# Probabilities times values in four column tiles of 32 tokens instead of two of 64, in a gated linear attention and expert layer

## What is computed

```python
A = jnp.einsum('bhntd,bhnsd->bhnts', q, k)
A = A * jnp.where(mask, jnp.exp(jnp.where(mask, dec, 0.0)), 0.0)
o_intra = jnp.einsum('bhnts,bhnsd->bhntd', A, v)
...
def step(S, inp):
    o_int = jnp.einsum('bhtd,bhde->bhte', qc * jnp.exp(gcc)[..., None], S)
...
o = o_intra + jnp.moveaxis(o_inter, 0, 2)
```

## Time and profile before

| | |
|---|---|
| median of 3 runs | 410.85 us (409.74 to 411.74) |
| the profiled execution, its time | 410.52 us |
| its span, first to last instruction | 408.6 us |
| mean granted TensorE clock | 0.991 |
| PE busy | 386.7 us, 3650 MATMULs |
| PEld busy | 337.1 us |
| DVE busy | 326.3 us |
| ACT busy | 304.5 us |
| POOL busy | 276.6 us |

### The profile page before, as it was taken

The page is one execution under the profiler, slowest core; times in us unless marked ns, Lnnn a source line. Parts: engine busy times, 40 slices in busy tenths (PEclk is TensorE's granted clock), DMA queues, the critical chain, the costliest instruction groups (busy, mean ns, idle before and its releaser), DMA issues.

```text
span 408.6 us, 13495 instructions
## 1 busy us (share of the span) xinstructions
PE 386.7 (95%) x3650; PEld 337.1 (83%) x3651; DVE 326.3 (80%) x868; ACT 304.5 (75%) x947; POOL 276.6 (68%) x237
## 2 busy tenths in 40 slices
PE   7988899999999999999999999899999999999990
PEld 6656788877788888888888878799999999999990
DVE  5989898999988898889888888667687687687750
ACT  4889998787887978797888887466666676666660
POOL 6012534268888888888888833178888888888884
PEclk9999999999999999999999999999999999999996
DMA  8846586464555445474655340145545555455530
GB/s 237 230 158 193 177 288 245 120 186 129 170 179 162 128 127 168 143 200 140 186 155 154 115 137 14 44 63 69 69 68 65 66 69 67 63 67 71 64 32 0
DMA packets 59096, 51.29 MB, mean 126 GB/s; under 512 B 7200, under 2 KB 51392, under 8 KB 59072
## 3 DMA queue, kind: packets, MB, share of 16 engines
q1 hardware_dynamic: 45936, 42.07, 36.0%
q0 software_dynamic: 12272, 8.54, 15.1%
q10 hardware_dynamic: 864, 0.40, 0.4%
HBM read 33.14 MB, written 18.30 MB: 126 GB/s over the span
## 4 chain that ended last, share of the span: by engine, by line
PE 80%; DVE 6%; ACT 4%; DMA 3%; issue 3%; POOL 2%; SPq 1%; ACTq 0%; DVEq 0%; POOLq 0%
PE psA L912 16%; PE psVG L900 16%; PE psVG L721 9%; PE psO L756 8%; PE psA L737 7%; PE psT L790 6%; PE psQK L709 6%; PE psT L782 4%; PE psKS L747 3%; PE psO L770 3%; ACT E L1080 2%; SPq L343 1%; DMA x_all<-in_L_attn_x_dram 1%; DMA gcB<-decay_rows 1%; PE psQK L891 1%
## 5 line engine op out<-in xcount | busy, mean ns | idle before, releaser
L579 POOL DMA_INDIRECT out_dram<-yw,sidx x71 | 115.0, 1619 | 29.1 <-issue 11.6
L538 POOL TENSOR_TENSOR rms<-msn,neg_half 128x8 f32<-128x8 f32 x32 | 53.3, 1665 | 48.4 <-DVE msn L1412 44.7
L1080 ACT ACTIVATE E<-gcB,ngc 128x128 f32<-128x128 f32 x256 | 78.5, 397 | 0.4 <-DMA gcB<-decay_rows 0.4
L544 POOL DMA_INDIRECT sorted_rows<-x_all,pos_i x64 | 65.2, 1019 | 14.4 <-issue 10.5
L531 POOL TENSOR_SCALAR_AFFINE_SELECT E<-E 128x1024 f32<-128x1024 f32 x32 | 35.7, 1115 | 33.5 <-ACT E L1080 33.2
L756 PEld LDWEIGHTS psO<-v_sb,pr 128*64 128x64 f32 x1024 | 39.8, 137 | 12.0 <-issue 4.1
L756 PE MATMUL psO<-v_sb,pr 128*64 128x64 f32 x1024 | 44.5, 225 | 2.7 <-DVE pr L1440 2.5
L1089 ACT ACTIVATE sq<-psO 128x512 f32<-128x512 f32 x32 | 19.1, 597 | 33.4 <-PE psO L756 33.4
L1440 DVE TENSOR_TENSOR pr<-psA,E 128x512 f32<-128x512 f32 x64 | 41.0, 682 | 0.2
L912 PE MATMUL psA<-xT_all,v_sb 128*128 x288 | 38.3, 276 | 0.5 <-issue 0.4
L900 PE MATMUL psVG<-xgT,gcB 128*128 128x128 f32 x288 | 38.6, 277 | 0.0
(11 more groups left out here) (197 smaller groups left out, 928.5 us busy)
## 6 DMA issues: line engine op xcount, KB each, us to landing
gcB<-decay_rows SPq DMA_DIRECT2D x32, 512.0 KB
sorted_rows<-blank SPq DMA_DIRECT2D x12, 396.0 KB, 5.5
xg<-sorted_rows SPq DMA_DIRECT2D x71, 66.0 KB
x_all<-in_L_attn_x_dram SPq DMA_DIRECT2D x16, 256.0 KB, 5.3
out_dram<-res SPq DMA_DIRECT2D x32, 128.0 KB
eqB<-decay_exp_rows SPq DMA_DIRECT2D x32, 64.0 KB
w1b<-in_L_ffn_w_dram SPq DMA_DIRECT2D x8, 256.0 KB
xT_all<-in_L_ffn_w_dram SPq DMA_DIRECT2D x32, 64.0 KB
```

What stands on the lines that cost most here:

```text
L538: nc.gpsimd.tensor_tensor(rms[:], msn[:], neg_half[:, 0:2 * H], ALU.pow).then_inc(rms_ready, 1)
L544: nc.gpsimd.indirect_dma_start(out=sorted_dram, out_offset=bass.IndirectOffsetOnAxis(ap=pos_i[:, t:t + 1], axis=0), in_=x_all[:, t, :], in ...
L579: nc.gpsimd.indirect_dma_start(out=out_rows, out_offset=bass.IndirectOffsetOnAxis(ap=sidx[j][:], axis=0), in_=yw[j][:], in_offset=None, bo ...
L1080: last = nc.scalar.activation(E[j][:, k, h * P:(h + 1) * P], gcB[j][:, k * H + h, :], ACT.Exp, bias=ngcf[:, bass.ds((s * 2 + k) * H + h, 1)])
```

## The change

A constant `QT = 4` is added, and the two loops over token tiles run over `QT` tiles of 32 tokens instead of 2 of 64. Each head of each chunk is then 4 matmuls instead of 2, and the state's part is 4 instead of 2; each still streams the same number of columns, against 32 columns of weights instead of 64. Nothing else is changed, waits and increments neither.

```diff
     LS = P // GT
+    QT = 4
...
                 for h in range(H):
-                    for c in range(2):
-                        t = k * SEQ + h % 2 * P + c * P // 2
-                        last = nc.tensor.matmul(psO[c * P // 2:(c + 1) * P // 2, k * HV + h * DV:k * HV + (h + 1) * DV], pr[:, h // 2, t:t + P // 2],
+                    for c in range(QT):
+                        t = k * SEQ + h % 2 * P + c * P // QT
+                        last = nc.tensor.matmul(psO[c * P // QT:(c + 1) * P // QT, k * HV + h * DV:k * HV + (h + 1) * DV], pr[:, h // 2, t:t + P // QT],
                                                 v_sb[j][:, k, h * DV:(h + 1) * DV], start=(k == 0 and h == 0), stop=(k == 1 and h == H - 1),
                                                 skip_group_check=True)
...
-                for c in range(2):
-                    nc.tensor.matmul(psO[c * P // 2:(c + 1) * P // 2, HV:2 * HV], qe[j][:, c * P // 2:(c + 1) * P // 2], S_sb[:],
+                for c in range(QT):
+                    nc.tensor.matmul(psO[c * P // QT:(c + 1) * P // QT, HV:2 * HV], qe[j][:, c * P // QT:(c + 1) * P // QT], S_sb[:],
                                      start=False, stop=False, skip_group_check=True)
```

## The result

The changed kernel took **428.7 us** (427.7 to 429.5, 4 runs) against 411.3 us (409.7 to 412.1, 4 runs) of the kernel before on the same chip: a ratio of 1.043, 95% interval 1.040 to 1.046. The forecast was 410.4 us and its range ended at 424, so both were missed.

What follows compares the result with a forecast made beforehand. PE's own time was taken as the bound; 29 ns gained on weight loads less 14 ns for a later end gave 0.5 us over 32 sequences, added starts costing nothing: 410.4 us, range 408.5 to 424.

Steps and rivals of the forecast that it cites:

- What bounds the kernel: In the attention stage PE's own time is the bound, so its gain or loss reaches the total almost one for one.
- Part (1): In each half of the outputs, 16 added MATMULs and 16 LDWEIGHTS cost zero; a step stays at 58 ns.
- (2): In the state's part, 4 more MATMULs and LDWEIGHTS cost zero, hidden under 208 ns of stream for each pass.
- (3): At a burst's first step, narrower weights load in 108 ns instead of 137, giving back 29 ns once a sequence.
- C: Rival: in the outputs' steps, 6 ns of overhead vanish with narrower weights, 3 us in all, 407 us; chance 0.10.
- rival B: Pauses in the outputs' long bursts come earlier or double, +2 to +13 us, 412.5 to 424 us; chance 0.35.

Runs made afterwards that it cites:

- second measurement: The unedited changed kernel timed again on another chip, against the kernel before there: 408.6 us, ratio 0.997 (0.995 to 0.999).
- 10: The kernel before (two tiles) with the state's part streamed as two pieces of 128 columns: 410.1 us, ratio 1.001.
- 12: The kernel before (two tiles), with GpSimd placing one tile, awaiting DVE's norming, masking, then placing two: 406.7 us, ratio 0.994.
- 15: The kernel before (two tiles) with 16 instead of 8 warm-up matmuls, which shifts TensorE's later code: 411.3 us, ratio 1.005.
- experiment 3: The changed kernel (four tiles) with GpSimd's mask after one placement and the other two placements behind it: 426.7 us, ratio 1.036.
- 4: The kernel before (two tiles) with GpSimd's mask after one placement and the other two placements behind it: 414.7 us, ratio 1.009.
- group 1: Four follow-up runs on one chip, without placing or with the mask moved, each on four and two tiles; the kernel before took 411.3 us there.

## Why the prediction was wrong, and where it was right

**What bounds the kernel**: right. What TensorE lost in the outputs came onto the total almost one for one: 20.8 us of longer periods, 20.1 between the medians.

**Part (1), added starts at nothing**: right. Quiet sequences on every chip show 32 MATMULs in 0.58 and 0.45 us; a step of four takes 56 ns, against 58 for a pair. The floor of about 25 ns between starts that the prediction cites from the Trainium skill (TensorE: Matmul & The Clock Gate, Back-to-back issue gap), and sets aside, would have made it 100; the trace's starts lie 7 ns apart. **(2)** and **(3)** were right too: 0.43 us for the state's part, loads of 111 ns. **C** had a grain of truth: a step got 2 ns shorter, of the 6 that it forecast. With part (3) the period is 0.07 us shorter (6.89 to 6.82). In 32 sequences this is 2.3 us, and the second measurement shows 0.7 us of it in the medians, its ratio's interval reaching to 0.995; where the other 1.6 went wasn't followed. So without the pauses the forecast of no change, 410.0 for 410.5, was right.

**The step that failed** is rival B: the sum put pauses at nothing, and B's own price ended at +13 us. Its sentence "If the pause ends at a given time, as much more of it is exposed: 0.8 us in each of the 16 sequences" was near the mechanism, for in most sequences of the slow trace the pause does end at a given time, that of GpSimd's indirect DMA. It mis-sized the count and the whole: not 16 sequences but the 21 in which GpSimd places rows, and not 13 us but 17 against before in those (165.9 - 148.8), 22.4 us of late MATMULs in all. Its 0.8 us for each sequence held in the 14 with one pause (0.69 to 0.86, 11.3 together); the seven with a second DMA, 1.0 to 2.0 us each and 11.0 together, it had not. I had read the pauses from s=11 on only, and left out s=7 to 10, where before has none; in the changed kernel the outputs of two of them run over 1.5 us late each. And the prediction spoke of "something that follows the count of instructions", with no look at what GpSimd does. The rows of the DMAs were in the trace of before: in all 21 sequences with placements an indirect DMA ran over the outputs, 15 of them have a pause, and the quiet sequence of the earlier trace rows, s=29, is one with 2 GpSimd operations instead of 6. But that trace didn't show it plainly. Six of the 21 have no pause, and the 15 pauses begin only 0.2 to 0.3 us after the DMA has ended. The worst, s=17:

```profile
156.71 0.99 POOL L544 DMA_INDIRECT sorted_rows<-x_all,pos_i  x1 [0.30 <-issue]
...
157.57 0.90 PE L756 MATMUL psO<-v_sb,pr 128*64 128x64 f32 x16
```

The DMA ends at 157.70, and the last two MATMULs, due from 157.98 on, come from 158.17 on. Had I still taken the DMA's length as the price, 1.0 to 1.25 us for each of 21, it would have been 21 to 26 us, an estimate with hindsight, around the 22.4 that were lost.

**What no reading of that trace could tell** is that the loss comes and goes with the chip. Before took 411.3 us in two groups of runs and 408.6 to 409.3 on four other chips. Its pauses sum to 2.1 us in its one trace, from the first measurement, which is about that difference; that it has none on the other four chips is inferred from its time there and from the traces of nearly the same kernels (10, 12 and 15). Where before has them, four tiles showed 22 us (first measurement) and, with most DMAs moved off, still 5 us against 0 for two tiles with the same edit (experiments 3 and 4). Where it seems to have none, four tiles have none.

**What is shown and what is not.** Shown: the loss is TensorE standing still in the outputs without waiting for an engine; each of its long stops in the changed kernel begins under an indirect DMA of GpSimd, and in 14 of 21 sequences ends with it, with no transfer under way; it moves with the DMA; without the DMAs it is absent on the chip of group 1, where experiment 3 has it; the same kernel on another chip has none. Only argued: that it is the supply of instructions that is held up, from the "issue" of the waits and from the fact that the MATMULs already there go on. The Trainium skill (Runtime: NRT & Kernel Launch, Instruction fetch mechanics) has each engine's instructions fetched by DMA in blocks, with the crossing of blocks mostly hidden. The traces have packets of such queues, but none in a pause from s=9 on, so they don't show a fetch as the cause. Open: why a pause under a second DMA outlasts it, and why those of the kernel before begin after the DMA's end; what differs between the chips, or between the places in memory that a program is given, or what else ran there. And whether the changed kernel takes 428.7 us on the chip of group 1, which was not measured: the 17 us themselves rest on one measurement.

## What to carry to other kernels

In this kernel, matmuls whose weights fill only part of the columns could be cut finer at no cost, as the tiles ran side by side (56 ns a step against 58), but it gains next to nothing where the stream sets the pace; and don't mix widths in one group. A denser stream of matmuls lost more to the same stops of TensorE here (22.4 us against 2.1), so look at what GpSimd does at the same moment, in every sequence and not in a sample, and price the overlap by the length of its DMAs. And before the cause of a loss is sought in the code, run the unedited changed kernel in each group of experiments: 16 runs without it led me to refute a theory that wasn't refuted, and to prove one that was false.

## What the runs showed of the hardware

- TensorE stood still for 0.4 to 0.75 us at a time while GpSimd was in an indirect DMA of 1.0 to 1.25 us, and for 0.3 to 1.0 us at a time where a second one followed, 22.4 us in all; on four other chips not once, in the same (one chip) and in nearly the same code.
- Starts of MATMULs in four different column tiles lie 7 ns apart, and a step of four with 64 columns takes 56 ns; one whole-width MATMUL of 64 columns takes a step of 112 ns.
- A change of the array's width costs: 0.91 us for two small full-width matmuls of two MATMULs each, and 0.10 to 0.12 us a sequence for halves of different widths.
- A DVE tensor_tensor between SBUF tiles took 2.12 instead of 0.68 us beside GpSimd's mask, and 0.68 beside its indirect DMA.
- The pauses go without any transfer: in the 14 sequences with one pause no DMA packet is under way in it.
